# A new order of entries for all engines of an attention and expert kernel on one core

## The reference

```
xn  = layernorm(x)
scores = xn @ qk @ xn.T / sqrt(128), causal mask
attn   = softmax(scores) @ xn @ ov
eid    = argmax(xn @ centroids.T)             # one of 8 experts for each token
alpha  = sigmoid(sum(xn * centroids[eid]))
xln    = layernorm(xn) * ln_g[eid] + ln_b[eid]
ffn    = relu(xln @ w1[eid] + b1[eid]) @ w2[eid] + b2[eid]    # 128 -> 512 -> 128
out    = x + attn + (xn + alpha * ffn)
```

## Time and profile before

| what | value |
|---|---|
| runs | 223.32, 222.75, 223.2 us; median 223.2 |
| span of the profiled execution | 223.1 us; 0.1 below the median, which is the time of the whole execution |
| TensorE busy | 206.3 us, 92% |
| VectorE busy | 175.5 us, 79% |
| ScalarE busy | 155.2 us, 70% |
| GpSimd busy | 154.3 us, 69% |
| granted clock of TensorE | full, but for a stretch in the first 20 us |

### The profile page before, as it was taken

One profiled execution on the slowest core, in us unless ns is written; L12 is line 12 of the kernel. 1 busy time (PEld: TensorE's weight loads), 2 busy tenths in 40 slices (PEclk: granted clock), 3 DMA queues, 4 the chain that ended last, 5 costly groups with the idle time before them and its releaser, 6 DMA issues.

```text
span 223.1 us, 6878 instructions
## 1 busy us (share of the span) xinstructions
PE 206.3 (92%) x2428; PEld 159.9 (72%) x2428; DVE 175.5 (79%) x448; ACT 155.2 (70%) x346; POOL 154.3 (69%) x230
## 2 busy tenths in 40 slices
...
GB/s 167 314 289 64 6 0 94 116 355 232 5 12 39 36 39 39 44 43 40 36 40 36 128 198 160 125 92 141 131 150 92 50 40 37 38 35 172 256 193 141
DMA packets 37601, 23.55 MB, mean 106 GB/s; under 512 B 12472, under 2 KB 34144, under 8 KB 37568
## 3 DMA queue, kind: packets, MB, share of 16 engines
...
q10 hardware_dynamic: 336, 0.14, 0.3%
...
## 4 chain that ended last, share of the span: by engine, by line
PE 77%; DVE 11%; ACT 4%; issue 4%; DMA 2%; SPq 1%; DVEq 0%; ACTq 0%
PE psum L1343 6%; PE psum L1300 6%; PE psum L1301 6%; PE psum L1302 6%; PE psum L1351 6%; PE psum L1344 6%; PE psum L1277 5%; PE psum L1460 4%; PE psum L1461 4%; PE psum L1462 4%; PE psum L1434 4%; PE psum L1436 4%; PE psum L1435 4%; PE psum L1260 3%; PE psum L1334 2%
## 5 line engine op out<-in xcount | busy, mean ns | idle before, releaser
L910 DVE TENSOR_TENSOR p_lo<-p_sb,p_hi 128x512 f16<-128x512 f32 (+1 forms) x68 | 42.0, 638 | 12.2 <-ACT p_sb L1050 12.0
L1044 ACT ACTIVATE p_hi<-psum 128x512 f16<-128x512 f32 (+1 forms) x68 | 37.1, 547 | 19.4 <-PE psum L1351 14.2
L1050 ACT ACTIVATE p_sb<-psum 128x512 f32<-128x512 f32 (+1 forms) x80 | 42.5, 539 | 6.8 <-PE psum L1334 6.7
L693 POOL DMA_INDIRECT sorted_y<-xn x39 | 38.1, 977 | 11.6 <-ACT xn L1174 5.5
L1018 DVE SCALAR_TENSOR_TENSOR h_lo<-psum,h_hi 128x512 f16<-128x512 f32 x39 | 26.8, 690 | 21.5 <-ACT h_hi L1166 18.7
L671 POOL MEMSET v_full<- 1x600 f32 x71 | 41.7, 588 | 0.0
L684 POOL DMA_INDIRECT sorted_x<-xr,pos x32 | 33.5, 1047 | 11.9 <-issue 11.4
L1166 ACT ACTIVATE h_hi<-psum 128x512 f16<-128x512 f32 x39 | 23.3, 597 | 21.0 <-PE psum L1436 19.2
L1343 PE MATMUL psum<-v_hi,p_hi 128*128 128x129 f16 x236 | 32.7, 220 | 1.2 <-DVE x_sb L927 1.2
L896 DVE TENSOR_REDUCE row_max<-psum 128x1 f32<-128x512 f32 x48 | 32.3, 682 | 1.6 <-PE psum L1277 1.1
L1344 PE MATMUL psum<-v_lo,p_hi 128*128 128x128 f16 x236 | 32.6, 219 | 0.0
...
## 6 DMA issues: line engine op xcount, KB each, us to landing
...
sorted_y<-xn POOLq DMA_INDIRECT x39
sorted_x<-xr,pos POOLq DMA_INDIRECT x32
```

Source lines behind the costliest of these rows:

```text
L693: pool.indirect_dma_start(out=sorted_y[:, :], out_offset=bass.IndirectOffsetOnAxis(ap=tokens, axis=0), in_=xs[:, t % SLOTS, 0:P], in_offse ...
L910: v.tensor_tensor(p_lo[:, u, off:GW], p_sb[:, u, off:GW], p_hi[:, u, off:GW], ALU.subtract).then_inc(s_plo, 1)
L1044: a.activation(p_hi[:, u, off:GW], bank[SCORE[n % R]][:, off:GW], ACT.Exp, scale=SCALE).then_inc(s_exph, 1)
L1050: a.activation(p_sb[:, u, off:GW], bank[SCORE[n % R]][:, off:GW], ACT.Exp, scale=SCALE).then_inc(s_exp, 1)
```

## The change

Only the text of `ORDER` differs. No entry is added or taken away, no instruction, shape or buffer changes; every engine does the same work in another order. Two lines of the diff, the first of the list:

```
 ORDER = entries("""
-VAR.0.1 VAR.1.2 BIASa LE.0.1 C0a AE.0 WU C0 C1 C2 T.0 W1.0 W1.1 BIAS RN.0.1 ROW.0.1 RN.1.2 MISC BASE.0 BASE.1 RN.2.3
+VAR.0.1 VAR.1.2 RN.0.1 LE.0.1 LE.1.2 C0a AE.0 C1a WU C0 C1 C2 T.0 T.1 W1.0 W1.1 ROW.0.1 MISC RN.1.2 RN.2.3 RN.3.4 RN.4.6
...
```

More of the change, by code:

```diff
@@ L119 @@
[L119 to L123, removed]
```

96 lines of the change are left out of this document (60 added, 36 removed).

## The result

The changed kernel takes 230.71 us (median of 4 runs, 229.85 to 231.68), the kernel before 223.26 in the same comparison. The ratio is 1.0321, with a 95% interval of 1.0287 to 1.0355: 3.2% slower, outside the forecast range, on the side of the slower rival.

The account below looks back on a forecast made before the run. VectorE was taken as nearest its limit in the head, then GpSimd's sends and stores as the chains. HI.0 at 121.0, plus 8.8 to SO.0, plus 90.3 behind it gave 220.1 us, range 218.2 to 224.2.

Parts of the forecast that it names:

- the slower rival: Pairs of score matmuls wait for exps between 66 and 126 us, so HI.0 stays at 126.2: 225.1 us, chance 0.17.
- The head: Up to CH.1: C2 starts 1.7 us earlier, VectorE's first set loses 4.05 of waits and doubling; CH.1 ends at 52.3.
- the first rival: The clock still falls around C2, leaving HI.0 at 121 to 123.3: 221.2 us, chance 0.15.
- From CH.1 to SC.0: Positions as before, 5.1 us; with W2l.3 to W2l.5 and S.5 on GpSimd ahead, 5.6: SC.0 at 57.9.
- The third rival: GpSimd's W2l and S.5 lock VectorE out beside CH and PL, SC.0 1 to 2 us later: 221 to 222, chance 0.11.
- From SC.0 to HI.0: GpSimd's sends, the issue and a 2.75 us landing of the first transposed load: 63.1 us, HI.0 at 121.0.
- the text's lower bound: TensorE's own stream allows HI.0 at 123.3 to 120 us, the earlier if the clock stays at 2.4 GHz.
- From HI.0 to SO.0: YS.0 stands behind RE.5, so the stores start 8.8 us after HI.0 instead of 5.4: 3.4 given back.
- The stores: GpSimd's 38 store steps from SO.0 take 66.15 us at 1.74 each, whatever TensorE does.
- Behind SO.38: Loads of y, additions and quotients after the last store; XL.67 behind Y.6 adds 0.6 us, XL.66 saves 0.5.
- The frame: Whole execution: forecast made against the profiled span of 223.1 us and 0.1 around it, the median of 223.2.
- the second rival: TensorE's stream loses the head's gain to waits for exps, HI.0 stays at 126.2: 225.1 us, chance 0.17.

Follow-up runs that it names:

- before_again: Kernel before, unchanged, run once for a second trace: 223.11 us, span 221.4.
- after_again: Changed kernel, unchanged, run once for a second trace: 230.34 us, span 228.6.
- e8: Kernel before with only the new order of the head: 225.11 us, ratio 1.0047.
- e11: Kernel before with the new order of the head, and BASE.6, BASE.4, BASE.5, BASE.7 ahead of W2l.0 on GpSimd: 223.27 us, ratio 1.0006.
- e10: Changed kernel with W2l.3, W2l.4, W2l.5 and S.5 on GpSimd behind SC.1 instead of ahead of SC.0: 230.59 us, ratio 1.0302.
- e12: Changed kernel with YS.0 behind RE.3, Sl.1 behind PL, W2l.3, S.5 to S.7, W2l.4 ahead of Vl.1, W2l.5 behind the sends: 224.24 us, ratio 1.0033.
- e4: Kernel before with YS.0 on ScalarE behind RE.5, nothing else changed: 225.89 us, ratio 1.0111.
- e6: Changed kernel with GpSimd's large operations moved away from CH, SIG and PL as far as possible, and Sl.1 behind PL: 229.79 us, ratio 1.0296.
- e1: Changed kernel with YS.0 on ScalarE behind RE.3 instead of behind RE.5: 226.61 us, ratio 1.0168.

## Why the prediction was wrong, step by step

Positions in us, from the traces; the forecast's from its text, the last two worked out from its terms.

| | forecast | before_again | after | after_again |
|---|---|---|---|---|
| C2 starts | 7.75 | 8.79 | 7.75 | 8.05 |
| CH.1 ends | 52.3 | 56.66 | 51.14 | 51.22 |
| SC.0 starts | 57.9 | 61.76 | 59.40 | 59.48 |
| HI.0 starts | 121.0 | 124.34 | 126.03 | 124.45 |
| SO.0 starts | 129.8 | 129.76 | 136.85 | 135.47 |
| SO.38 starts | 195.9 | 197.31 | 202.86 | 203.15 |
| last quotient ends | 217.7 | 219.10 | 227.26 | 226.33 |

Between the forecast of 220.1 and the profiled execution of 231.26 lie 11.2 us: 1.2 less up to CH.1's end, then 2.7 more up to SC.0, 3.5 up to HI.0, 2.0 up to SO.0, 0.1 less in the stores, 2.6 more behind SO.38, and 1.6 of the frame.

- **The head.** Right, and mis-sized only to the cautious side. ROW.1.2 took 1.11 and the clock stayed at its upper level (1.00 from 10 to 15 us), so the first rival did not come. But the credit is not all the head's: with the new head and the old order behind it CH.1 ends at 57.3 and 57.2 (e8, e11), no earlier than in before_again, though X.0 starts 1.9 earlier. The 5.5 against before_again needs the order behind the head as well.
- **From CH.1 to SC.0** was sized at 5.6 and took 8.3. The step that failed is "By the path of the positions it is as before, 5.1 us": W2l.3 to W2l.5 and S.5 were costed by GpSimd's own time only. That time came out (S.5 ends 5.6 behind CH.1), but the positions, stretched beside these operations, took 7.2 and SC.0 another 1.0. e10 shows it: without the four operations there SC.0 starts 5.5 behind CH.1. The third rival had the mechanism, with a price of 1 to 2 us where SIG and PL lost 2.8, and a chance of 0.11.
- **From SC.0 to HI.0** was sized at 63.1 and took 66.6 and 65.0: a wait of SC.4 for Sl.1 (1.5 in the first trace), sends that took longer on average (1097 ns against 1047 on the two pages, 1.6 for 32), and a landing 0.5 later. Why the sends took longer stays open. The forecast did not look at Sl.1, which had never been waited for; with Sl.1 behind PL the wait is gone (e12). TensorE was ready at 120.0, as the text's lower bound said.
- **From HI.0 to SO.0** was sized at 8.8 and took 10.8 and 11.0. The term itself was right (8.64 in e4 and e6 at the upper clock). The 2.2 above it are the clock, which fell in TensorE's 6 us of standing still. The text looked for a fall of the clock only in the head.
- **The stores**: 66.0 in the first trace, as forecast, and 67.7 in the second, so that "1.74 each, whatever TensorE does" holds to 1.7 us only.
- **Behind SO.38** 24.4 and 23.2 to the last quotient, against 21.8 in before_again; forecast 21.8. XL.67 behind Y.6 was costed at 0.6, as work that moves. It is a wait: stores that end late hold Y.6, XL.67 and then TensorE (2.08). e1 has no such stop.
- **The frame** was off by 1.6: the sum set the positions of one trace against the median of other runs, with 0.1 us around the span. In the traces taken later the execution is 1.7 longer than its span.

So HI.0 came no earlier, as in the second rival, yet not by its mechanism: the sends were late, while TensorE waited. With HI.0 unmoved, YS.0's place was a net loss: it starts the stores 3.2 later, which cost 2.5 in e4. The clock and the tail came on top.
